# Top-ten stage and decoder layer in one program block; three weights scaled during the experts

## The chip, the cores and the metric

The kernel runs on 1 core of one Trainium2 chip. The metric is device time in microseconds, the median of several executions; less is better. One execution of the kernel was also recorded by the hardware profiler, and the rows below come from it.

## The reference

Four layers are applied one after the other to x of shape (16, 128, 256), with a context of the same shape, all in float32:

```
x = L0(x, ctx)   # self-attention, cross-attention (16 heads), then a mixture of experts: top 2 of 8
x = L1(x, ctx)   # per batch: score every row, take the ten best, attend from them to ctx,
                 #   write the ten results back in place of the ten rows
x = L2(x, ctx, mask)   # decoder layer:
    h, kv = rmsnorm(x, ln1), rmsnorm(ctx, ln1)
    q, k, v = h @ Wq, kv @ Wk, kv @ Wv          # 16 query heads, 4 key heads of 64
    q, k = rope(q), rope(k)
    hidden = x + softmax(q k^T / 8 + mask) v @ Wo
    x = hidden + (silu(n @ Wgate) * (n @ Wup)) @ Wdown,   n = rmsnorm(hidden, ln2)
x = L3(x, ctx)   # attention with ternary weights, residual
```

The gain ln1 multiplies the rows of Wq, Wk and Wv, and ln2 those of Wgate and Wup. The kernel multiplies these weights by their gains once, in SBUF, and then norms rows by their root mean square alone.

## The kernel before

The kernel is written by hand: every engine (PE, ACT, DVE, POOL, SP) has its own list of instructions, kept in order by counting semaphores. A `with nc.Block(...)` opens a stretch in which each engine runs its own function; at its end the engines meet. `end_turn()` (L244) adds an `all_engine_barrier` (L246) that also clears the semaphores so that their counts start again from zero. The stages:

- Self-attention and cross-attention of L0 with the router between them (block at L644). Its scatter of row ids is 32 indirect DMAs from POOL (L1292).
- Experts (block at L1434): 39 blocks of 128 rows. SP streams 2 MB of weights for each block and, at blocks 8, 13, 18, 23 and 28 (`grouped_at`), loads five of the decoder's six weights. POOL gathers the rows of block j + 2 (L1142) and scatters the results of block j - 2 (L1150), both indirect DMAs.
- Top-ten stage (block at L1632): four groups g of four batches. For each group PE computes `scores`, DVE takes `maxima`, PE turns the maxima, DVE subtracts them from the queries, PE computes `scores_turned`, ACT takes `exps`, PE computes `products`, DVE divides, PE makes `rows_out`, DVE adds a bias, PE's `put_back` spreads the ten rows and DVE's `replace` writes them into `xres`. Two PSUM banks serve the small jobs in the order of the list `in_turn`: a job's bank must have been read out (`tok_claim`) before the next job on it starts. POOL only multiplies four weights by their gains in this stage (L1658). SP loads the experts' rows, then `wq2`, and, once the last `products` are done, the mask (L1651). `end_turn()` follows.
- Decoder layer (block at L2080): a pipeline over 16 batches in slots t. Batch b's input stage is `stats_in` (DVE), `rms_in` (POOL), `scale_in` (DVE), `turn_in` (PE), `in_copy` (ACT), `queries` twice and `keys_values` (PE), `rope_queries`, `rope_keys` (DVE), `values` (ACT), and `rope_sums` (POOL). It runs in slots t = -3 to -1 for the first batches, with nothing else beside it. Then `scores` of batch 0 (L2096) opens slot 0. `end_turn()` follows.
- L3's attention, and the stores.

Of the kernel before, what the change touches and what calls it, by code (L numbers as in the profile page):

```python
# [17 lines left out]
P = 128  # L18
# [46 lines left out]
def build(nc, A, out):  # L65
    with ExitStack() as ctx:
# [72 lines left out]
        def view(at, shape):  # L139
# [3 lines left out]
            if len(shape) == 1:  # L143
# [63 lines left out]
        mask2 = w_sa[:, :, :].rearrange("p c n -> p (c n)").rearrange("p (b k) -> p b k", b=B)  # L207
# [9 lines left out]
        ld = {n: sem("ld_" + n) for n in ("x", "ctx", "small", "sa", "ca", "l1", "l3", "l2", "ids", "xn", "mask", "fc2b")}  # L217
# [10 lines left out]
        names = ["s_full", "st_full", "mt_full", "nd_full", "a_full", "b_full", "c_full", "a_free", "b_free", "c_free", "max_ok", "sub_ok", "p_ok", "o_ok",  # L228
                 "row_full", "row_ok", "bv_ok", "bias_ok", "pad_ok", "hx_ok", "hc_ok", "q_full0", "q_full1", "q_free0", "q_free1", "chain", "pchain", "const", "stats", "rstd_ok", "xn_ok",
                 "cn_ok", "summed", "divided", "scaled", "values_ok", "scored", "masked", "shifted", "maxed", "probs", "turned", "pt_ok", "biased",  # L230
                 "multiplied", "roped", "act_ok", "fc1_full", "fc1_free", "fc2_full", "y_ok",
                 "turned_in", "xb_ok", "routed", "picked_in", "taken", "measured", "keys_ok",
                 "counted", "scattered", "xs_ok", "colb_ok", "gat_ok", "exp_ok", "gates_ok",
                 "s0_full", "s1_full", "s2_full", "s3_full", "s0_free", "s1_free", "s2_free", "s3_free",
                 "stats_mid", "rstd_mid", "mid_ok",
                 "row_stats", "rows_ok", "chosen_ok", "rows_at", "totals", "ids_ok", "tables", "moe_chain", "kv_full", "kv_free", "tok_qk_ok",
                 "tok_b_full", "tok_c_full", "tok_b_free", "tok_c_free", "tok_colb_ok", "tok_gat_ok", "tok_p_ok", "tok_s_full", "tok_max_ok", "tok_mt_full", "tok_sub_ok", "tok_st_full", "tok_o_ok", "tok_nd_full", "tok_put_full", "tok_bv_ok", "tok_pad_ok", "tok_chain", "put_full", "late_rstd"]
# [93 lines left out]
        def load_grouped(sp, n):  # L331

            tile = {"wq2": wq2, "wkv2": wkv2, "wo2": wo2, "wg2": wg2, "wu2": wu2, "wd2": wd2}[n]
            sp.dma_start(tile, A[n].rearrange("(c p) n -> p c n", p=P)).then_inc(ld["l2"], 16)
# [1296 lines left out]

        with nc.Block(no_gpsimd_drain=True) as block:  # L1632
            @block.sync
            def _(sp):
# [24 lines left out]

            @block.tensor  # L1660
            def _(pe):
# [139 lines left out]
                for g in range(G):  # L1801
                    if g > 0:
                        put_back(g - 1)
                    maxima_turned(g)
                    if g + 1 < G:
                        score_rows(g + 1)
                    scores_turned(g)
                    if g + 1 < G:
# [7 lines left out]
                    products(g)  # L1816
                    if g + 1 < G:
# [10 lines left out]
            def _(act):  # L1828
# [60 lines left out]
                for g in range(G):  # L1889
                    exps(g)  # L1890
                    if g + 1 < G:
# [14 lines left out]
            def _(dve):  # L1906
                link = chained(dve, M["tok_chain"])

# [76 lines left out]
                def replace(g):  # L1985
                    dve.wait_ge(M["tok_put_full"], g + 1)
                    for j in range(GB):
                        b = g * GB + j
                        nc.vector.scalar_tensor_tensor(out=xres[:, b, :], in0=xres[:, b, :], scalar=keep[:, b:b + 1],
                                                       in1=S[j][:, 0:D], op0=ALU.mult, op1=ALU.add)  # L1990
# [9 lines left out]
                for g in range(G):  # L2000
# [16 lines left out]
        A4 = H // NKV  # L2017
        w2 = 12288
        masked_tile = SP
        turned_probs = PT  # L2020
        roped_q = view(w2, [2, 2, A4, P])
        roped_k = view(w2 + 2048, [2, 2, P])
        values2 = view(w2 + 2560, [2, NKV, HD])
        normed_in = view(w2 + 3072, [2, 2, D])
        normed_inT = view(w2 + 4096, [2, 2 * C, P])
        normed_mid = view(w2 + 5120, [D])
        normed_midT = view(w2 + 5376, [C, P])
        gated = view(w2 + 5632, [FC, P])
        heads_out = view(w2 + 6656, [FC, P])
        q_cos, q_sin = [w_ca[:, c, :].rearrange("p (h a n) -> p h a n", h=2, a=A4) for c in range(2)]  # L2030
        k_cos, k_sin = [w_l1[:, 0, k * D:(k + 1) * D].rearrange("p (h n) -> p h n", h=2) for k in range(2)]
        st_mid, mv_mid, ve_mid, rstd_mid = small[:, 0:6], small[:, 6:8], small[:, 8:9], small[:, 9:10]

        SLOT_JOBS = [("wo", -1, "a"), ("qa", 1, "b"), ("qb", 1, "c"), ("kv", 1, "a"), ("xt", -1, 0), ("at", 2, 1),
                     ("g0", -1, 2), ("u0", -1, 3), ("g1", -1, 0), ("u1", -1, 1), ("pv0", 0, "a"), ("pv1", 0, "b"), ("d", -1, "c")]
        JOB_BANK = {0: banks[0], 1: banks[1], 2: banks[2], 3: banks[3], "a": banks[5], "b": banks[6], "c": banks[7]}
        JOB_FULL = {0: M["s0_full"], 1: M["s1_full"], 2: M["s2_full"], 3: M["s3_full"],
                    "a": M["a_full"], "b": M["b_full"], "c": M["c_full"]}
        JOB_FREE = {0: M["s0_free"], 1: M["s1_free"], 2: M["s2_free"], 3: M["s3_free"],
                    "a": M["a_free"], "b": M["b_free"], "c": M["c_free"]}  # L2040
        job_at, n_jobs = {}, {h: 0 for h in JOB_BANK}
        for t in range(-2, B + 1):
            for name, ahead, home in SLOT_JOBS:
                if 0 <= t + ahead < B:
                    job_at[name, t + ahead] = (home, n_jobs[home])
                    n_jobs[home] += 1

        def job_claim(pe, name, b):

            home, k = job_at[name, b]  # L2050
            if k > 0:
                pe.wait_ge(JOB_FREE[home], k)
            if home in range(4) and 0 <= slot_of(name, b) < B:
                pe.wait_ge(M["masked"], 4 * slot_of(name, b) + home + 1)
            return JOB_BANK[home]

        def slot_of(name, b):
            return b - next(ahead for n, ahead, _ in SLOT_JOBS if n == name)

        def job_done(name, b):  # L2060
            return JOB_FULL[job_at[name, b][0]]

        def job_moved(name, b):
            return JOB_FREE[job_at[name, b][0]]

        def await_done(eng, name, b):

            home, k = job_at[name, b]
            eng.wait_ge(JOB_FULL[home], k + 1)
            return JOB_BANK[home]  # L2070

        def await_job_moved(eng, name, b):

            home, k = job_at[name, b]
            eng.wait_ge(JOB_FREE[home], k + 1)

        def is_batch(b):
            return 0 <= b < B

        with nc.Block(no_gpsimd_drain=True) as block:  # L2080
            @block.tensor
            def _(pe):

                def scores(b):
                    pe.wait_ge(M["roped"], 4 * (b + 1))
                    if b > 0:
                        pe.wait_ge(M["masked"], 4 * b)
# [10 lines left out]
                    ins.then_inc(M["scored"], 1)  # L2098
# [456 lines left out]
```

## Time and profile before

| | us |
|---|---|
| median of 3 runs | 1445.94 (1444.47 to 1445.95) |
| the profiled execution: its own time / its span | 1450.84 / 1449.1 |
| PE busy in the span | 1298.5 (90%) |
| DVE / ACT / POOL busy | 677.1 / 621.4 / 427.8 |

Starts are microseconds from the start of the span. PE means matmuls, PEld the loading of their weights, SPq, POOLq and so on the sequencers of these engines. What stands in brackets behind a row is the idle time of that engine before it and whose instruction ended it. A row of a window has its start and end, its length, the busy time and count of PE, PEld, DVE, ACT and POOL, the granted clock of PE (1.00 is 2.4 GHz, 0.50 is 1.2 GHz), the busy share of the DMA engines and GB/s. By start times the experts end and the top-ten stage begins at 679; its last instruction starts at 818.36; the decoder's first at 830.30; L3's attention begins at about 1283.

### The profile page before, as it was taken

What the parts mean: (1) busy time and instruction counts of PE and PEld (TensorE: products, weight loads), DVE (VectorE), ACT (ScalarE), POOL (GpSimd) and SP (SyncE); (2) the same over time, 40 slices, a digit from 0 to 9 for tenths busy, and PEclk for the clock granted to TensorE, in tenths of its full rate; (3) what the DMA queues carried; (4) which work ended last, traced back from release to release, by engine and by line L of the source; (5) the groups of instructions that cost most, each with busy time, mean ns of one, the idle gap of its engine ahead of it and who ended that gap; (6) DMA issues with size and microseconds to landing.
All of it is one profiled execution on the core that took longest, in us unless ns stands there. A gap on an engine that the chain in (4) does not pass through costs nothing. (4 is left out here: it accounts for less than half of the span.)

```text
span 1449.1 us, 34173 instructions
## 1 busy us (share of the span) xinstructions
PE 1298.5 (90%) x13946; PEld 1058.8 (73%) x13946; DVE 677.1 (47%) x1457; ACT 621.4 (43%) x1444; POOL 427.8 (30%) x549
## 2 busy tenths in 40 slices
PE   4899999976899999999687379999999999788997
PEld 2566666655689999997566268888888888666665
DVE  3676777766322000001753255455464453336666
ACT  2444555421545455553121046455455565334442
POOL 3224445253223222221500044334334242132200
PEclk9999999997899999999567589999999999999999
DMA  8000000000589999996300100000000000000000
GB/s 293 2 2 2 2 2 16 9 16 23 157 294 333 339 354 351 356 332 211 101 2 2 30 1 1 2 2 1 1 1 1 2 1 1 1 1 2 17 16 31
DMA packets 80042, 120.11 MB, mean 83 GB/s; under 512 B 12112, under 2 KB 62544, under 8 KB 79760
## 3 DMA queue, kind: packets, MB, share of 16 engines
q1 hardware_dynamic: 73840, 106.62, 21.9%
q0 software_dynamic: 4768, 10.26, 2.0%
q8 instruction: 112, 1.84, 0.5%
q10 hardware_dynamic: 1280, 1.04, 0.2%
q14 instruction: 42, 0.34, 0.1%
HBM read 108.43 MB, written 9.48 MB: 81 GB/s over the span
## 5 line engine op out<-in xcount | busy, mean ns | idle before, releaser
L1529 ACT ACTIVATE w_ca<-scores,fc1b 128x128 f32<-128x128 f32 x312 | 114.3, 367 | 140.1 <-PE scores L1484 118.9
L921 ACT ACTIVATE reg<-scores 128x1024 f32<-128x1024 f32 x96 | 93.0, 1021 | 168.8 <-PE scores L688 151.1
L1484 PEld LDWEIGHTS scores<-reg 128*128 128x128 f32 x1248 | 146.7, 194 | 6.9 <-DMA reg<-in_fc 2.7
L1484 PE MATMUL scores<-reg 128*128 128x128 f32 x1248 | 147.7, 277 | 3.6 <-DMA reg<-in_fc 1.5
L1494 PE MATMUL bank<-reg,w_ca 128*128 128x256 f32 x624 | 141.1, 379 | 0.3 <-DVE small L1554 0.3
L1015 DVE TENSOR_REDUCE reg<-scores 128x8 f32<-128x1024 f32 x96 | 113.0, 1219 | 57.9 <-PE scores L678 49.6
L2215 ACT ACTIVATE reg<-reg,mx 128x128 f32<-128x128 f32 x256 | 99.1, 389 | 83.8 <-DVE mx L2395 83.4
L1563 DVE TENSOR_TENSOR reg<-bank,reg 128x256 f32<-128x256 f32 x39 | 16.6, 425 | 241.4 <-PE bank L1494 226.4
L2304 POOL TENSOR_TENSOR reg<-reg,rden 128x512 f32<-128x512 f32 x64 | 66.5, 1040 | 210.7 <-DVE rden L2400 210.6
L1494 PEld LDWEIGHTS bank<-reg,w_ca 128*128 128x128 f32 x624 | 115.6, 190 | 14.5 <-DVE small L1554 0.3
L2131 PE MATMUL scores<-reg 128*128 128x128 f32 x1024 | 122.3, 279 | 0.5 <-ACT reg L2238 0.5
L2131 PEld LDWEIGHTS scores<-reg 128*128 128x128 f32 x1024 | 119.7, 196 | 0.7 <-ACT reg L2238 0.7
L2124 PE MATMUL bank<-reg 128*128 128x256 f32 x512 | 118.8, 385 | 0.8 <-issue 0.8
L2124 PEld LDWEIGHTS bank<-reg 128*128 128x128 f32 x512 | 94.7, 190 | 26.6 <-issue 13.2
L1036 DVE RECIPROCAL reg<-bank 128x256 f32<-128x256 f32 x48 | 84.2, 1754 | 33.2 <-PE bank L703 30.0
L861 ACT ACTIVATE reg<-bank,qk_bias,shape_c 128x512 f32<-128x512 f32 x96 | 69.5, 778 | 56.4 <-PE bank L661 56.0
L1150 POOL DMA_INDIRECT expert_out<-reg,block_ids_of x39 | 38.5, 986 | 151.5 <-DVE reg L1563 85.6
L2131 PE MATMUL bank<-reg 128*128 128x128 f32 x640 | 78.2, 279 | 0.7 <-ACT reg L2245 0.7
L2131 PEld LDWEIGHTS bank<-reg 128*128 128x128 f32 x640 | 76.5, 195 | 1.9 <-ACT reg L2245 1.1
L2422 DVE TENSOR_TENSOR reg<-scores,reg 128x512 f32<-128x512 f32 x32 | 22.1, 692 | 109.8 <-PE scores L2131 109.8
L688 PEld LDWEIGHTS scores<-reg 32*128 32x128 f32 x1536 | 48.2, 189 | 30.5 <-issue 30.4
L678 PEld LDWEIGHTS scores<-reg 32*128 32x128 f32 x1536 | 48.7, 188 | 29.2 <-ACT reg L921 22.9
(272 smaller groups left out, 2324.3 us busy)
## 6 DMA issues: line engine op xcount, KB each, us to landing
reg<-in_fc SPq DMA_DIRECT2D x78, 1024.0 KB
reg<-expert_out SPq DMA_DIRECT2D x16, 256.0 KB, 3.0
xres<-in_x SPq DMA_DIRECT2D x4, 512.0 KB, 11.3
ctxr<-in_ctx SPq DMA_DIRECT2D x1, 2048.0 KB, 15.5
w_l<-in_w_l SPq DMA_DIRECT2D x2, 1024.0 KB, 12.5
routed_rows<-reg SPq DMA_DIRECT2D x8, 256.0 KB
out<-xres SPq DMA_DIRECT2D x8, 256.0 KB, 2.6
w_sa<-in_w_sa SPq DMA_DIRECT2D x1, 1024.0 KB, 8.4
```

What stands on the lines that cost most here:

```text
L678: ins = nc.tensor.matmul(S[r][:, (2 * s + c) * P:(2 * s + c + 1) * P], Qs[rows_of(r), (b // GB) % 2, s, c, batch(b)], Ks[rows_of(r), (b // ...
L861: ins = nc.scalar.activation(dst[:, g % 2, s, m, :], bank[:, :], ACT.Identity, scale=scale[:, s:s + 1], bias=bias[:, s, m:m + 1])
L921: ins = nc.scalar.activation(PT2[:, t % 2, 2 * half:2 * half + 2, :, :, :].rearrange("p r s c q -> p (r s c q)"), scores4[:, 2 * half:2 * ...
L1015: ins = nc.vector.tensor_reduce(mxpad.rearrange("p (c n d) -> p n c d", c=C, d=DH)[:, 4 * half:4 * half + 4, :, 0], scores4[:, 2 * half:2 ...
L1036: link(nc.vector.reciprocal(rd, banks[4][:, 2 * P:4 * P]))
L1484: ins = nc.tensor.matmul(S[n % 4][:, 0:P], up_w8[j % 2][:, c, f * P:(f + 1) * P], xbT[:, j % 2, c, :], start=(c == 0), stop=(c == C - 1))
L1494: ins = nc.tensor.matmul(T[j % 2][:, 0:D], h1[:, j % 2, f, :], down_w8[j % 2][:, f, :], start=(f == 0), stop=(f == FC - 1))
L1529: nc.scalar.activation(h1[:, j % 2, f, :], S[n % 4][:, 0:P], ACT.Gelu, bias=fc1b[:, bass.ds(e * FC + f, 1)]).then_inc(M["fc1_free"], 1)
L2124: ins = nc.tensor.matmul(bank[:, 0:D], src[:, f, :], w[:, f, :], start=(f == 0), stop=(f == FC - 1))
L2131: ins = nc.tensor.matmul(bank[:, k * P:(k + 1) * P], w[:, c, w0:w0 + P], src[:, c, :], start=(c == 0), stop=(c == C - 1))
L2215: ins = nc.scalar.activation(v[:, a, :], v[:, a, :], ACT.Exp, bias=cols_of(mx, n)[:, a:a + 1], accum_out=cols_of(psum, n)[:, a:a + 1])
L2304: nc.gpsimd.tensor_tensor(v, v, spread(rden, n), ALU.mult).then_inc(M["scaled"], 1)
```

## The change

1. The decoder's functions move into the top-ten stage's block, behind it on each engine; the block's end and `end_turn()` between them go. So the decoder gets semaphores of its own (`l2_...`), and PE waits for the last `replace` (`tok_back`) before `scores` of batch 0.
2. The input stage of batches 0 and 1 and the queries, keys and values of batch 0 are made inside the top-ten stage: `stats_in` of batches 0 to 2 in group 2, `scale_in` of 0 and 1 at its end, and the rest in group 3. Five jobs are put into `in_turn` ahead of the last `y`. Some tiles get other places for this (`normed_in`, `q_cos`, `gated`, the mask).
3. `wkv2`, `wg2` and `wu2` are multiplied by their gains on POOL in the experts' blocks 33 to 35; only `wq2` stays in the top-ten stage.
4. The mask's load moves to just behind the load of `wq2`.

```diff
-        mask2 = w_sa[:, :, :].rearrange("p c n -> p (c n)").rearrange("p (b k) -> p b k", b=B)
+        mask2 = view(0, [B, P])
...
+        gains_at = {33: (wkv2, "ln1"), 34: (wg2, "ln2"), 35: (wu2, "ln2")}
...  # experts, gpsimd, inside the loop over j, behind gather_rows and scatter_rows
+                    if j in gains_at:
+                        w, gain = gains_at[j]
+                        pool.wait_ge(ld["l2"], 16 * len(grouped_at))
+                        for c in range(C):
+                            nc.gpsimd.tensor_scalar(w[:, c, :], w[:, c, :], col(gain, c), None, ALU.mult).then_inc(M["tok_gains"], 1)
...
+            if g + 1 == G:
+                in_turn += [("at", 0), ("at", 1), ("qa", 0), ("qb", 0), ("kv", 0)]
             in_turn += [("y", g)]
...  # top-ten, sync
                 load_grouped(sp, "wq2")
+                sp.dma_start(mask2, A["mask"].rearrange("b q k -> q b k")).then_inc(ld["mask"], 16)
                 for g in range(1, G):
                     expert_rows_in(g)
-                sp.wait_ge(M["tok_nd_full"], G)
-                sp.dma_start(mask2, A["mask"].rearrange("b q k -> q b k")).then_inc(ld["mask"], 16)
...  # top-ten, gpsimd
-                pool.wait_ge(ld["l2"], 16 * 6)
-                for w, gain in ((wq2, "ln1"), (wkv2, "ln1"), (wg2, "ln2"), (wu2, "ln2")):
-                    for c in range(C):
-                        nc.gpsimd.tensor_scalar(w[:, c, :], w[:, c, :], col(gain, c), None, ALU.mult)
+                pool.wait_ge(ld["wq2"], 16)
+                for c in range(C):
+                    nc.gpsimd.tensor_scalar(wq2[:, c, :], wq2[:, c, :], col("ln1", c), None, ALU.mult).then_inc(M["tok_gains"], 1)
...  # top-ten, tensor
                     if g > 0:
                         put_back(g - 1)
+                    if g + 1 == G:
+                        l2_turn_in(pe, 0)
+                        l2_turn_in(pe, 1)
                     maxima_turned(g)
                     if g + 1 < G:
                         score_rows(g + 1)
+                    if g + 1 == G:
+                        pe.wait_ge(M["tok_gains"], 4 * C)
+                        l2_queries(pe, "qa", 0, 0)
                     scores_turned(g)
+                    if g + 1 == G:
+                        l2_queries(pe, "qb", 0, 1)
...
                     products(g)
+                    if g + 1 == G:
+                        l2_keys_values(pe, 0)
...  # top-ten, scalar
+                    if g + 1 == G:
+                        l2_in_copy(act, 0)
+                        l2_in_copy(act, 1)
                     exps(g)
+                    if g + 1 == G:
+                        l2_values(act, 0)
...  # top-ten, vector
+                    if g == G - 2:
+                        for b in range(3):
+                            l2_stats_in(dve, l2_link[0], b)
+                    if g + 1 == G:
+                        l2_rope_queries(dve, 0, 0)
+                        l2_rope_queries(dve, 0, 1)
                     divide(g)
...
                     out_rows(g)
+                    if g == G - 2:
+                        l2_scale_in(dve, 0)
+                        l2_scale_in(dve, 1)
+                    if g + 1 == G:
+                        l2_rope_keys(dve, 0)
                 replace(G - 1)
-        end_turn()
...
-        with nc.Block(no_gpsimd_drain=True) as block:
             @block.tensor
             def _(pe):
...
-                pe.wait_ge(ld["l2"], 16 * 6)
-                for t in range(-2, B + 1):
+                pe.wait_ge(M["tok_back"], 1)
+                pe.wait_ge(M["tok_o_ok"], G)
+                for t in range(B + 1):
...  # decoder, gpsimd: rope_sums, loop still from t = -3
+                    if b == 0:
+                        pool.wait_ge(M["tok_st_full"], 3)
+                        pool.wait_ge(M["tok_nd_full"], 3)
```

The functions `l2_turn_in`, `l2_queries`, `l2_keys_values`, `l2_in_copy`, `l2_values`, `l2_stats_in`, `l2_scale_in`, `l2_rope_queries` and `l2_rope_keys` are the decoder's own ones of before, with the same instructions, moved out so that both stages can call them.

## Rows read from the trace of the kernel before

**Rows 1.** Windows over the top-ten stage, the gap and the decoder.

```profile
680.00:820.00 140.00, 104.85 (x1839) 84.09 (x1838) 71.82 (x218) 27.57 (x45) 20.64 (x9) 0.68 0.16 48
820.00:846.00 26.00, 8.89 (x56) 8.13 (x60) 7.40 (x23) 1.58 (x3) 6.11 (x14) 0.63 0.00 1
846.00:1282.00 436.00, 419.98 (x3692) 368.56 (x3692) 207.39 (x474) 227.26 (x714) 151.01 (x243) 0.99 0.01 1
```

**Rows 2.** Timeline of all engines, from the last top-ten instruction to the decoder's first scores.

```profile
818.36 1.66 DVE L1989 SCALAR_TENSOR_TENSOR xres<-xres,reg,scores 128x256 f32<-128x256 f32 x4 [1.36 <-PE scores L1780]
...
830.30 0.43 DVE L2359 BATCH_NORM_STATS2 st<-xres 128x6 f32<-128x256 f32 x1 [10.29 <-PEq L246]
...
835.55 6.25 PE L2131 MATMUL bank<-reg 128*128 128x128 f32 x40 [0.69 <-ACT reg L2245]
...
845.76 3.59 PE L2096 MATMUL scores<-reg 32*128 32x128 f32 x64 [2.65 <-POOL reg L2327]
```

**Rows 3.** The barrier's line L246 in 815:835, count, min/median/max ns.

```profile
L246 POOLq DRAIN  x1: 9057/9057/9057, 820.3 to 820.3; - x1
```

**Rows 4.** The same line in 1200:1300, behind the decoder.

```profile
L246 POOLq DRAIN  x1: 34/34/34, 1282.1 to 1282.1; - x1
...
  DVE st L992: 1.4, 1
```

**Rows 5.** Timeline of PE in the last top-ten group.

```profile
799.11 7.05 PE L1744 MATMUL scores<-w_ca,reg 32*128 32x32 f32 x128 [2.19 <-DVE w_ca L1968]
808.22 1.93 PE L1759 MATMUL bank<-w_sa,reg 128*32 128x32 f32 x128 [2.06 <-ACT w_sa L1877]
...
814.68 1.86 PE L1772 MATMUL bank<-w_l,reg 128*128 128x256 f32 x4 [2.41 <-DVE reg L1976]
817.05 1.24 PE L1780 MATMUL scores<-reg 32*128 32x256 f32 x8 [0.52 <-DVE reg L1983]
```

**Rows 6.** Timeline of PE, the same shapes and the decoder's projections elsewhere.

```profile
790.36 1.10 PE L1772 MATMUL bank<-w_l,reg 128*128 128x256 f32 x4 [1.31 <-DVE reg L1976]
...
863.22 2.07 PE L2096 MATMUL scores<-reg 32*128 32x128 f32 x64
...
868.77 3.73 PE L2131 MATMUL bank<-reg 128*128 128x128 f32 x32
```

**Rows 7.** Windows: the decoder's first projections, and the last `scores_turned`.

```profile
799.00:806.00 7.00, 6.89 (x128) 6.89 (x128) 0.06 (x1) 0.00 (x0) 0.00 (x0) 0.50 0.01 2
...
835.50:839.00 3.50, 3.45 (x17) 3.45 (x18) 0.62 (x2) 0.00 (x0) 0.68 (x1) 0.53 0.00 0
```

**Rows 8.** Timeline of DVE in groups 2 and 3, and of its input stage.

```profile
788.00 1.76 DVE L1975 RECIPROCAL reg<-bank 128x256 f32<-128x256 f32 x1 [15.08 <-PE bank L1764]
...
793.34 2.36 DVE L1958 TENSOR_REDUCE reg<-scores 128x8 f32<-128x1024 f32 x2 [1.41 <-PE scores L1726]
...
812.31 1.76 DVE L1975 RECIPROCAL reg<-bank 128x256 f32<-128x256 f32 x1 [13.25 <-PE bank L1764]
...
833.01 0.35 DVE L2369 TENSOR_SCALAR reg<-xres,rstd 128x256 f32<-128x256 f32 x1 [1.68 <-POOL rstd L2298]
```

**Rows 9.** Timeline of ACT in group 3.

```profile
806.23 1.94 ACT L1877 ACTIVATE w_sa<-scores 128x1024 f32<-128x1024 f32 x2 [15.64 <-PE scores L1744]
```

**Rows 10.** Timeline of POOL: block 35's scatter, the last gather, the four weights' gains.

```profile
647.16 0.99 POOL L1150 DMA_INDIRECT expert_out<-reg,block_ids_of  x1 [3.32 <-DVE reg L1563]
650.13 0.96 POOL L1142 DMA_INDIRECT reg<-routed_rows,block_ids_of  x1 [1.98 <-PE bank L1473]
...
690.98 20.40 POOL L1658 TENSOR_SCALAR reg<-reg,cols 128x1024 f32<-128x1024 f32 x8 [10.74 <-DMA reg<-in_wq]
```

**Rows 11.** PE timeline: the last gathered block is turned. DMA view: a scatter's landing.

```profile
663.48 0.38 PE L1473 MATMUL bank<-ident,reg 128*128 128x128 f32 x2
...
expert_out<-reg,block_ids_of POOLq DMA_INDIRECT x39, 5.9
```

**Rows 12.** Window: the experts' rows and wq2 arriving.

```profile
688.00:690.00 2.00, 1.81 (x9) 1.25 (x7) 1.43 (x4) 0.75 (x2) 0.00 (x0) 1.00 0.98 390
```

More of the change, by code:

```diff
@@ L214, in build @@
         Q = banks[6:8]
-        ld = {n: sem("ld_" + n) for n in ("x", "ctx", "small", "sa", "ca", "l1", "l3", "l2", "ids", "xn", "mask", "fc2b")}
+        ld = {n: sem("ld_" + n) for n in ("ctx", "small", "sa", "ca", "l1", "l3", "l2", "wq2", "ids", "xn", "mask", "fc2b")}
         stored = sem("stored")
@@ L1630, in keys_of @@
             return slice(j * P, (j + 1) * P)
+        A4 = H // NKV
+        w2 = 12288
+        masked_tile = SP
+        turned_probs = PT
+        roped_q = view(w2, [2, 2, A4, P])
+        roped_k = view(w2 + 2048, [2, 2, P])
+        values2 = view(w2 + 2560, [2, NKV, HD])
+        normed_in = view(2048, [2, 2, D])
+        normed_inT = view(3072, [2, 2 * C, P])
+        normed_mid = view(w2 + 3072, [D])
+        normed_midT = view(w2 + 3328, [C, P])
+        k_cos, k_sin = [view(w2 + 3584 + D * k, [2, P]) for k in range(2)]
@@ new lines, in build @@
+        q_cos, q_sin = [view(w2 + 4096 + 1024 * k, [2, A4, P]) for k in range(2)]
+        gated, heads_out = [w_ca[:, c, :].rearrange("p (f n) -> p f n", f=FC) for c in range(2)]
+        st_mid, mv_mid, ve_mid, rstd_mid = small[:, 0:6], small[:, 6:8], small[:, 8:9], small[:, 9:10]
+        SLOT_JOBS = [("wo", -1, "a"), ("qa", 1, "b"), ("qb", 1, "c"), ("kv", 1, "a"), ("xt", -1, 0), ("at", 2, 1),
+                     ("g0", -1, 2), ("u0", -1, 3), ("g1", -1, 0), ("u1", -1, 1), ("pv0", 0, "a"), ("pv1", 0, "b"), ("d", -1, "c")]
@@ new lines, in build, with job_claim @@
+        IN_TOP_TEN = [("at", 0), ("at", 1), ("qa", 0), ("qb", 0), ("kv", 0)]
+        for t in range(-2, B + 1):
+            for name, ahead, home in SLOT_JOBS:
+                if 0 <= t + ahead < B and (name, t + ahead) not in IN_TOP_TEN:
+                    job_at[name, t + ahead] = (home, n_jobs[home])
+                    n_jobs[home] += 1
+        def job_claim(pe, name, b):
+            if (name, b) in IN_TOP_TEN:
+                return tok_claim(pe, (name, b))
+            home, k = job_at[name, b]
+            if k == 0 and home in ("a", "c"):
+                h = tok_bank.index(JOB_BANK[home])
+                pe.wait_ge(tok_free[h], sum(1 for n in tok_at if tok_at[n][0] == h))
+            if k == 0 and home == "b":
+                pe.wait_ge(M["tok_sub_ok"], G)
+            if k > 0:
+                pe.wait_ge(JOB_FREE[home], k)
+            if home in range(4) and 0 <= slot_of(name, b) < B:
+                pe.wait_ge(M["l2_masked"], 4 * slot_of(name, b) + home + 1)
+            return JOB_BANK[home]
@@ new lines, in slot_of, with job_done, job_moved, await_done @@
+        def slot_of(name, b):
+            return b - next(ahead for n, ahead, _ in SLOT_JOBS if n == name)
+        def job_done(name, b):
+            if (name, b) in IN_TOP_TEN:
+                return tok_done((name, b))
+            return JOB_FULL[job_at[name, b][0]]
+        def job_moved(name, b):
+            if (name, b) in IN_TOP_TEN:
+                return tok_moved((name, b))
+            return JOB_FREE[job_at[name, b][0]]
+        def await_done(eng, name, b):
+            if (name, b) in IN_TOP_TEN:
+                return tok_await(eng, (name, b))
+            home, k = job_at[name, b]
+            eng.wait_ge(JOB_FULL[home], k + 1)
+            return JOB_BANK[home]
@@ new lines, in await_job_moved, with is_batch, l2_project @@
+        def await_job_moved(eng, name, b):
+            if (name, b) in IN_TOP_TEN:
+                return tok_await_moved(eng, (name, b))
+            home, k = job_at[name, b]
+            eng.wait_ge(JOB_FREE[home], k + 1)
+        def is_batch(b):
+            return 0 <= b < B
+        cos = [rope[:, 0, :].unsqueeze(1).to_broadcast([P, n, P]) for n in (A4, 2)]
+        sin = [rope[:, 1, :].unsqueeze(1).to_broadcast([P, n, P]) for n in (A4, 2)]
+        def l2_project(pe, name, b, w, w0s, src):
+            bank = job_claim(pe, name, b)
+            for k, w0 in enumerate(w0s):
+                for c in range(C):
+                    ins = nc.tensor.matmul(bank[:, k * P:(k + 1) * P], w[:, c, w0:w0 + P], src[:, c, :],
+                                           start=(c == 0), stop=(c == C - 1))
+            return ins
@@ new lines, in l2_queries, with l2_keys_values @@
+        def l2_queries(pe, name, b, half):
+            await_job_moved(pe, "at", b)
+            l2_project(pe, name, b, wq2, [(2 * a + half) * P for a in range(A4)], normed_inT[:, b % 2, 0:C, :])\
+                .then_inc(job_done(name, b), 1)
+        def l2_keys_values(pe, b):
+            bank = job_claim(pe, "kv", b)
+            for k in range(2):
+                for c in range(C):
+                    nc.tensor.matmul(bank[:, k * P:(k + 1) * P], wkv2[:, c, k * P:(k + 1) * P], normed_inT[:, b % 2, C + c, :],
+                                     start=(c == 0), stop=(c == C - 1))
+            for c in range(C):
+                ins = nc.tensor.matmul(bank[:, D:2 * D], normed_inT[:, b % 2, C + c, :], wkv2[:, c, D:2 * D],
+                                       start=(c == 0), stop=(c == C - 1))
+            ins.then_inc(job_done("kv", b), 1)
@@ new lines, in l2_turn_in, with l2_values @@
+        def l2_turn_in(pe, b):
+            pe.wait_ge(M["l2_xn_ok"], b + 1)
+            bank = job_claim(pe, "at", b)
+            for k in range(2):
+                for c in range(C):
+                    ins = nc.tensor.transpose(bank[:, (C * k + c) * P:(C * k + c + 1) * P],
+                                              normed_in[:, b % 2, k, c * P:(c + 1) * P], ident[:])
+            ins.then_inc(job_done("at", b), 1)
+        def l2_values(act, b):
+            bank = await_done(act, "kv", b)
+            if b == 0:
+                act.wait_ge(M["tok_st_full"], 3)
+            if b >= 2:
+                await_done(act, "pv1", b - 2)
+            nc.scalar.activation(values2[:, b % 2, :, :], bank[:, D:2 * D].rearrange("p (h d) -> p h d", d=HD), ACT.Copy)\
+                .then_inc(M["l2_values_ok"], 1)
@@ L2028, in build @@
[L2028 to L2035, printed above, removed]
@@ L2260, in out_copy @@
                         .then_inc(job_moved(f"pv{q}", b), 1)
-                for t in range(-2, B + 1):
+                for t in range(B + 1):
                     now, before_now, after_now = is_batch(t), is_batch(t - 1), is_batch(t + 1)
@@ L2345, in _ @@
             def _(dve):
[L2346 to L2348 removed]
+                link = l2_link[0]
                 def add_rows(name, b):
@@ L2425, in _ @@
                 dve.wait_ge(ld["mask"], 16)
-                for t in range(-3, B + 2):
+                for t in range(B + 2):
                     now, before_now, after_now = is_batch(t), is_batch(t - 1), is_batch(t + 1)
```

277 lines of the change are left out of this document (102 added, 175 removed).

## Prediction

> **What bounds the kernel now.** Read the windows by stage first [rows 1]. In the decoder PE is busy 419.98 of 436.00 us at a granted clock of 0.99: it is the bound there, and the change gives PE the same matmuls. In the top-ten stage PE is busy 104.85 of 140.00 us, all other engines less: a chain through PE, DVE and ACT sets the time. From 820 to 846 PE is busy 8.89 of 26.00 us and nothing else is busier: that stretch is what the change attacks.
>
> Next the timeline of all engines there [rows 2]. The last `replace` ends at 818.36 + 1.66 = 820.02. DVE's next instruction starts 10.29 us later, held by the barrier. Then the input stage of the first batches runs as a bare chain, and `scores` of batch 0 start at 845.76. So 845.76 - 820.02 = 25.74 us lie between the two stages: 10.28 of barrier and 15.46 of filling.
>
> Third, what the barrier consists of [rows 3]: POOL's DRAIN takes 9.06 us of it. The barrier behind the decoder, at the same line, has a DRAIN of 0.03 us, and DVE goes on after 1.4 us [rows 4]. So the 9 us don't belong to a barrier as such. What differs: the one at 820 is the first DRAIN that POOL executes behind its indirect DMAs (32 of the router, 39 gathers, 39 scatters); behind it POOL issues none. By 820 POOL had been idle since 711.38, the end of the gains [rows 10].
>
> **Part 1, one block.** It removes this barrier, 10.28 us. But one stays behind the decoder, and now that is the first behind the indirect DMAs. I take it that the DRAIN's 9.06 us move there, exposed as at 820, because all engines meet before it: its 0.03 becomes 9.06, +9.03. The ends: 0, if the 9 us belong to the place, and +9.03. Of the two I take the upper one, as nothing in the rows ties the time to the place and one thing ties it to what went before.
>
> The Trainium skill (page "VectorE: DVE Perf Modes", section "The DRAIN you can't avoid") says that the DRAINs of a kernel's boilerplate take about 12 ns, constant, on all five engines. The POOL row of 9057 ns is far from it [rows 3], that of 34 ns near [rows 4]. By this rule nothing would come back behind the decoder, and the gain would be 9 us more than by the row. The measurement decides for the row; rival (a) has the same outcome.
>
> **Part 2, the input stage inside the top-ten stage.** It removes the 15.46 us of filling. What it adds, place by place:
>
> DVE, group 2: `stats_in` of three batches is twelve small instructions. I bound them by the first at 0.43 us each, 5.2 us [rows 2]; 15.08 us of idleness stand before `divide` [rows 8]. Nothing. POOL's `rms_in` is free there. `scale_in` of two batches, 4 x 0.35 = 1.4 us [rows 8], stands between `out_rows` and `maxima`, where DVE is idle 1.41 us: nothing, with no reserve.
>
> PE, group 3: eight transposes before `maxima_turned`. The eight matmuls of the decoder's projections at full clock take 8 x 0.117 = 0.9 us [rows 6], and PE is idle 2.19 us before `scores_turned` [rows 5], in part because DVE does `replace` first. Nothing. Then `qa`, 16 matmuls, in the same idle time. At full clock 16 x 0.117 = 1.9 us; at 1.2 GHz the decoder's first projections ran 17 in 3.50 us, 0.206 each, so 3.3 us [rows 7]. PE has 2.19 - 0.9 = 1.3 us left: `scores_turned` start 0.6 to 2.0 us later. I take 2.0, as the clock stood at 0.50 through all of `scores_turned` [rows 7].
>
> `qb` lies in the 2.06 us in which PE waits for `exps` [rows 5]: 1.9 us fits, 3.3 costs 1.2. I take 0.6. `kv`, eight matmuls of 128 and four of 256 columns, lies in the 2.41 us before `rows_out` [rows 5]; at full clock it takes 8 x 0.117 + 4 x 0.23 = 1.9 us (0.23 as twice 0.117), at half clock 3.5 us and then costs 1.1. I take 0.5.
>
> ACT: two `in_copy` lie in 15.64 us of idleness [rows 9]; nothing. DVE: four `rope_queries` of the projections' results lie in the 13.25 us before the last `divide` [rows 8]; nothing. `rope_keys` lies in the 1.36 us before `replace` [rows 2]; its two instructions of 256 columns are bounded by 2 x 0.43; nothing. POOL's `rope_sums` ends behind `rope_keys` while DVE still does `replace` (1.66 us): nothing. The new wait of PE on `tok_back` holds nothing that could go earlier: behind it stand `scores`, which need the same PSUM banks. I take 0.2 us from the end of `replace` to the first matmul.
>
> The clock can pay this back. The same instructions at half and full clock [rows 5, 6]: `rows_out` 1.86 against 1.10, `scores` 3.59 [rows 2] against 2.07. In group 3 PE now has more to do between its waits, so the clock falls later or not at all: between 0 and 0.76 + 1.52 = 2.3 us for these two, and for `scores_turned`, never at full clock here, between 0 and half of 7.05, 3.5. I take half of each, 2.9 us. Added 2.0 + 0.6 + 0.5 + 0.2 = 3.3; given back 2.9; the net is +0.4, between -5.0 (0.6 + 0.2 - 2.3 - 3.5) and +4.5 (2.0 + 1.2 + 1.1 + 0.2).
>
> The Trainium skill (page "TensorE: Matmul & The Clock Gate", section "Part 1: The HAM clock gate") says that the slow clock is the default and sustained activity releases it. It would put the net at the lower end, -5.0 and 1424.7 in all, since `qa` and `qb` are dense work; the rows show 0.50 over a `scores_turned` with PE busy 6.89 of 7.00 us [rows 7], so being busy alone did not raise it.
>
> **Part 3, gains during the experts.** The eight instructions took 20.40 us for seven halves of 1024 columns, 2.9 us each [rows 10]; `wkv2` is 2.9, `wg2` and `wu2` 5.8 us each. In the top-ten stage they were off the path: PE waited for none. In the experts they stand before the next gather. The last is the tightest: block 35's scatter, at 647.16 before, comes some 0.4 us later, the gains of `wu2` follow for 5.8 us and gather 38 is issued at about 654.3 instead of 650.13. It is needed when PE turns its rows at 663.48 [rows 11], 9.2 us later. I count nothing; without this cover a late gather stalls PE by as much as it is late. The weights' loads themselves are where they were. In the top-ten stage POOL no longer works beside DVE from about 697 to 711; I take nothing for that, between -2 and 0.
>
> **Part 4, the mask.** 1 MB more, behind `wq2` and before the rows of group 1. Group 0's rows are issued before it, but arrive beside `wq2` while the DMA engines are busy 0.98 at 390 GB/s [rows 12]: 1 MB at that rate is 2.7 us. The first scores of the top-ten stage wait for these rows. SP itself issues one DMA more before group 1's rows, which are needed only after group 0's; nothing else stands behind it on SP. I take 0.5, between 0 and 2.7.
>
> **Sum.** -25.74 + 9.03 + 0.4 + 0.5 = -15.8 us. The profiled execution took 1450.84 us, 1.74 more than its span; it becomes 1435.0. It lies 4.9 us above the median of the runs, 1445.94, and the gain is in fixed waits, so the median becomes 1430.1.
>
> **Rivals.** (a) The DRAIN doesn't come back: -15.8 - 9.0 = -24.8, 1421.1. For it: the decoder's POOL work then lies between the indirect DMAs and the DRAIN, and whatever it waits for may have passed. Against it: at 820 the gains and over 100 us of idleness lay between, and it still took 9 us. (b) The DRAIN moves, and the work put into group 3 runs at the slow clock with nothing paid back and the mask in full: -25.74 + 9.03 + 4.5 + 2.7 = -9.5, 1436.4. For it: the clock of 0.50 in `scores_turned`. Against it: the projections' own window shows 0.53 and their 40 matmuls together took 6.25 us [rows 2], less than 40 x 0.206, so the clock rose within them. (c) The moved gains stall the experts, and the kernel gets slower. Gather 38 has 9.2 us from issue to need; its transfer may take the 5.9 us of a scatter, as large [rows 11], so 3.3 remain. The gains are 14.5 us in all. If beside the DMA stream POOL took k times as long, the last gather would be late by at most 14.5 (k - 1) - 3.3: it eats the 15.8 us from k = 2.3, and at k = 3 the time is 1445.94 - 15.8 + 25.7 = 1455.8. For it: their time beside the matmuls' and DMAs' traffic is not in any row. Against it: beside a busy DVE they took 2.9 us each.
>
> **Chances.** The forecast (DRAIN moves, net near zero): 0.70. (a) 0.14, (b) 0.12, (c) 0.03; 0.01 for no change. The range reaches from rival (a)'s time to just short of (b)'s: 1420 to 1436. A measurement of this kernel tells 0.2%, 2.9 us, from no change. Faster: 0.70 + 0.14 + 0.12 = 0.96; same 0.01; slower 0.03.
>
> **What would show it.** In the profile of the changed kernel: no barrier between `replace` and `scores`, and under 1 us between them; a POOL DRAIN of about 9 us at the barrier behind the decoder, and L3's attention starting about 16 us earlier than at 1283 (25 if rival (a) holds and the DRAIN is short). `scores_turned` of group 3 starting 0.6 to 2.0 us later after `put_back`; if the clock column reads 1.00 there, the lower end of the net holds. The experts' end at the same time as before, within 0.5 us; if it is later, (c). If the gap between `replace` and `scores` is over 3 us, a wait that I took as covered isn't: POOL's `rope_sums`, or `out_rows` behind `qb`'s bank.

## The result and the profile after

The changed kernel took 1425.24 us (median, 1423.89 to 1428.53), the kernel before, on the same chip, 1445.2 (1440.54 to 1445.95): ratio 0.9872, 95% interval 0.9844 to 0.9900, 20.0 us less. The forecast was 1430.1 us, 15.8 less. The profiled execution of the changed kernel took 1426.36 us with a span of 1424.5.

Timeline of the changed kernel, all engines, where [rows 2] showed the gap: the last `replace`, then `scores` of batch 0. Columns as there.

```profile
807.10 1.66 DVE L2170 SCALAR_TENSOR_TENSOR xres<-xres,reg,scores 128x256 f32<-128x256 f32 x4 [0.18 <-PE scores L1945]
...
808.81 3.06 PE L2223 MATMUL scores<-reg 32*128 32x128 f32 x64 [1.78 <-DVE xres L2170]
```

`replace` ends at 808.76 and PE goes on at 808.81. Of the 25.74 us between the stages 0.05 are left. The barrier's line behind the decoder, in 1200:1300, answers to [rows 4]:

```profile
L237 POOLq DRAIN  x1: 9057/9057/9057, 1246.1 to 1246.1; - x1
...
  DVE st L983: 10.3, 1
```

The DRAIN has moved there at its full 9057 ns, and DVE now waits 10.3 us instead of 1.4. The last top-ten group answers to [rows 5]:

```profile
790.27 0.71 PE L1945 MATMUL scores<-reg 32*128 32x256 f32 x8 [2.54 <-DVE reg L2139]
790.91 1.09 PE L1741 MATMUL bank<-ident,reg 128*128 128x128 f32 x8
791.84 0.38 PE L1899 MATMUL bank<-ident,reg 128*128 128x128 f32 x2
792.35 2.02 PE L1716 MATMUL bank<-reg 128*128 128x128 f32 x16
794.30 3.77 PE L1909 MATMUL scores<-w_ca,reg 32*128 32x32 f32 x128
798.00 2.05 PE L1716 MATMUL bank<-reg 128*128 128x128 f32 x16
800.13 1.26 PE L1924 MATMUL bank<-w_sa,reg 128*32 128x32 f32 x126
...
802.23 1.16 PE L1729 MATMUL bank<-reg 128*128 128x128 f32 x8
803.22 1.03 PE L1732 MATMUL bank<-reg 128*128 128x256 f32 x4
804.70 1.10 PE L1937 MATMUL bank<-w_l,reg 128*128 128x256 f32 x4 [0.45 <-DVE reg L2157]
806.32 0.71 PE L1945 MATMUL scores<-reg 32*128 32x256 f32 x8 [0.52 <-DVE reg L2164]
```

Each added job (L1741 the transposes, L1716 `qa` and `qb`, L1729 and L1732 `kv`) stands where PE was idle. Their matmuls of 128 columns took 0.126 to 0.145 us each (a group's time by its count), at a granted clock of 1.00. What came after ran at that clock too: `scores_turned` took 3.77 us instead of 7.05. Windows of 2 us over PE (busy time and count, clock, DMA share, GB/s) show why. In the kernel before, PE did little ahead of `scores_turned` (799.11), and the clock fell:

```profile
794.00:796.00 2.00, 0.16 (x4) 1.00 0.00 0
796.00:798.00 2.00, 0.93 (x10) 0.95 0.00 0
798.00:800.00 2.00, 0.89 (x18) 0.50 0.00 0
```

In the changed kernel PE is busy there, and the clock falls only behind the wait for the last `replace`, within the decoder's first `scores` (808.81):

```profile
792.00:794.00 2.00, 1.88 (x18) 1.00 0.03 8
794.00:796.00 2.00, 2.00 (x65) 1.00 0.00 0
...
808.00:810.00 2.00, 1.19 (x36) 0.92 0.00 0
810.00:812.00 2.00, 2.00 (x37) 0.50 0.04 8
```

The gains on POOL were one block of 20.40 us in [rows 10]. Two of the three weights that moved, among the gathers and scatters of the experts (timeline of POOL, blocks 34 to 36):

```profile
636.72 5.68 POOL L1459 TENSOR_SCALAR reg<-reg,cols 128x1024 f32<-128x1024 f32 x2
642.57 1.01 POOL L1133 DMA_INDIRECT reg<-routed_rows,block_ids_of  x1 [0.17 <-issue]
643.88 1.01 POOL L1141 DMA_INDIRECT expert_out<-reg,block_ids_of  x1 [0.30 <-issue]
644.93 5.69 POOL L1459 TENSOR_SCALAR reg<-reg,cols 128x1024 f32<-128x1024 f32 x2
650.79 1.03 POOL L1133 DMA_INDIRECT reg<-routed_rows,block_ids_of  x1 [0.18 <-issue]
```

The profiled executions cut at the same instructions (starts and ends from the timelines, in us):

| stretch | before | after | difference |
|---|---|---|---|
| start to the experts' first block | 386.61 | 384.01 | -2.60 |
| experts | 291.19 | 289.63 | -1.56 |
| to group 3's first `put_back` | 118.04 | 116.63 | -1.41 |
| to the end of the last `replace` | 24.18 | 18.49 | -5.69 |
| to `scores` of batch 0 | 25.74 | 0.05 | -25.69 |
| to the decoder's last instruction on DVE | 436.01 | 436.95 | +0.94 |
| to L3's first | 1.37 | 10.33 | +8.96 |
| to the end of the span | 165.96 | 168.41 | +2.45 |

In the profiles of the kernels below the start takes 379.5 to 389.2, the experts 289.4 to 295.1, the decoder 433.2 to 440.4 and the last stretch 165.9 to 168.7 us, though their edits hardly touch these stretches. The third stretch takes 116.45 to 118.81 us in those whose top-ten stage is the changed kernel's up to there. So the differences in the first three rows and in the decoder's and the last are no shown effects of the change. What repeats in both profiles of the changed kernel is 18.49, 0.05 and 10.33.

### The profile page after: what moved, and what is told of

It reads as the page before. It is cut to its first block and busy times, and to the rows that moved or that the text cites. A ratio compares the mean times of both kernels' runs of the same rounds, so it can differ in the third digit from the quotient of the medians.

```text
span 1424.5 us, 34151 instructions
## 1 busy us (share of the span) xinstructions
PE 1292.7 (91%) x13946; PEld 1057.5 (74%) x13946; DVE 673.3 (47%) x1457; ACT 621.6 (44%) x1444; POOL 428.5 (30%) x549
## 5 line engine op out<-in xcount | busy, mean ns | idle before, releaser
L1491 PE MATMUL bank<-reg,w_ca 128*128 128x256 f32 x624 | 141.1, 380 | 0.3 <-DVE small L1551 0.3
L1491 PEld LDWEIGHTS bank<-reg,w_ca 128*128 128x128 f32 x624 | 115.8, 191 | 14.3 <-DVE small L1551 0.3
L1716 PE MATMUL scores<-reg 128*128 128x128 f32 x1024 | 122.4, 279 | 0.5 <-ACT reg L2330 0.5
L1716 PEld LDWEIGHTS scores<-reg 128*128 128x128 f32 x1024 | 119.8, 196 | 0.7 <-ACT reg L2330 0.7
L2251 PE MATMUL bank<-reg,w_ca 128*128 128x256 f32 x512 | 118.8, 386 | 0.8 <-issue 0.8
L2251 PEld LDWEIGHTS bank<-reg,w_ca 128*128 128x128 f32 x512 | 94.9, 190 | 26.4 <-issue 13.2
L2474 DVE TENSOR_TENSOR w_ca<-scores,w_ca 128x512 f32<-128x512 f32 x32 | 22.1, 692 | 109.8 <-PE scores L1716 109.8
L669 PE MATMUL scores<-reg 32*128 32x128 f32 x1536 | 59.9, 295 | 11.2 <-ACT reg L912 10.8
L679 PE MATMUL scores<-reg 32*128 32x128 f32 x1536 | 57.7, 287 | 12.4 <-DVE reg L1006 12.4
```

The costliest lines, as they stand in the source:

```text
L669: ins = nc.tensor.matmul(S[r][:, (2 * s + c) * P:(2 * s + c + 1) * P], Qs[rows_of(r), (b // GB) % 2, s, c, batch(b)], Ks[rows_of(r), (b // ...
L679: ins = nc.tensor.matmul(S[r][:, (2 * s + c) * P:(2 * s + c + 1) * P], Ks[rows_of(r), (b // GB) % 2, s, c, batch(b)], Qs[rows_of(r), (b // ...
L1491: ins = nc.tensor.matmul(T[j % 2][:, 0:D], h1[:, j % 2, f, :], down_w8[j % 2][:, f, :], start=(f == 0), stop=(f == FC - 1))
L1716: ins = nc.tensor.matmul(bank[:, k * P:(k + 1) * P], w[:, c, w0:w0 + P], src[:, c, :], start=(c == 0), stop=(c == C - 1))
L2251: ins = nc.tensor.matmul(bank[:, 0:D], src[:, f, :], w[:, f, :], start=(f == 0), stop=(f == FC - 1))
```

## The experiments

All ratios are to the kernel before, timed on the same chip, with their 95% intervals. Three groups of four kernels ran, each with the kernel before beside it: `after_again`, `after_drain`, `before_drain` and `after_nofill` (before: 1452.85 us); `qa_late`, `warm`, `warm_drain` and `drains` (1450.92); `gains_late`, `mask_late`, `warm2_drain` and `drains2` (1449.71). The changed kernel ran in the first group alone; those of the other groups are set beside it by their ratios.

**after_again**: the changed kernel once more.

> The changed kernel itself, beside the others on one chip. Both theories: about 20 us under the kernel before, as in its first runs (1425.24 against 1445.2).

Measured: 1430.31 us, 0.9843 (0.9823 to 0.9863), 22.5 us less. With the first result the gain is 20 to 23 us.

**after_drain**: is it the place or what went before?

```diff
                 # top-ten, gpsimd, behind the gains of wq2
+                nc.gpsimd.drain()
```

> The changed kernel with one more DRAIN on POOL, behind the gains of wq2, where POOL is idle for about 75 us. Theory A (the 9 us belong to the first DRAIN behind indirect DMAs): the new DRAIN takes about 9.06 us under cover, the one of the barrier behind the decoder 0.03 us, and the kernel is 9 us faster than the changed one, 29 under before. Theory B (they belong to the barrier's place, or to the first barrier): the barrier keeps its 9.06 us and the time stays that of the changed kernel.

Measured: 1420.54 us, 0.9801 (0.9764 to 0.9838), 9.8 us under `after_again`; but the runs spread from 1414.77 to 1433.18 us and the two intervals overlap, so it is the profile that decides. The barrier behind the decoder, the new DRAIN, and the gains ahead of it:

```profile
L237 POOLq DRAIN  x1: 41/41/41, 1246.4 to 1246.4; - x1
...
  DVE st L983: 1.4, 1
...
L1824 POOLq DRAIN  x1: 14917/14917/14917, 688.4 to 688.4; - x1
...
688.46 5.78 POOL L1823 TENSOR_SCALAR reg<-reg,cols 128x1024 f32<-128x1024 f32 x2 [11.48 <-DMA reg<-in_wq]
```

The new DRAIN also counts the gains that run while it waits. They end at 688.46 + 5.78 = 694.24, it ends at 703.3: 9.1 us of its own. Decoder's end to L3 takes 1.40 us again. Theory A holds and B falls.

**before_drain**: the same line behind the four gains in the kernel before.

> The kernel before with the same DRAIN behind the four gains in the top-ten stage. Theory A: its barrier at 820 shrinks from 10.3 to about 1.4 us and the kernel gets 9 us faster (ratio 0.994). Theory B: no change.

Measured: 1446.17 us, 0.9962 (0.9943 to 0.9982), 6.7 us less. The gap between the stages is 17.30 us instead of 25.74, 8.4 less, with a DRAIN of 41 ns in it. The last group took 25.01 us instead of 24.18 in this profile, so 7.6 us remain of it, within the interval of the time (2.6 to 8.3 us less). The 9 us expected were too many by little.

**drains and drains2**: what sets the 9 us?

```diff
                 # drains: behind the router's last scatter; drains2: experts, block 8, behind the memset
+                nc.gpsimd.drain()
                 # both: behind the gains of wq2 (in drains twice)
+                nc.gpsimd.drain()
```

> The changed kernel with a DRAIN on POOL behind the router's 32 indirect DMAs, and two more, one behind the other, behind the experts' 78 (after the gains of wq2). Theory A1 (9 us for the first DRAIN behind any indirect DMAs): about 9, 9 and 0.03 us, the work that runs ahead of each not counted. A2 (only the first DRAIN of the program): 9, 0.03, 0.03. A3 (so much for each DMA): 2.6, 6.4, 0.03.

> The changed kernel with a DRAIN on POOL in the experts' block 8 (50 indirect DMAs behind it) and one behind the gains of wq2 (60 more). If the time goes by the number of indirect DMAs since the last DRAIN (9.06 / 110 = 0.082 us each, as the 6.4 us behind 78 suggest), the second takes 60 x 0.082 = 4.9 us behind the gains; if it is fixed, 9; if it goes by what is still in flight, near 0.

Measured: 1424.92 and 1415.65 us, of one execution each, so no gain is read from them. The table has the DRAIN's end less the end of POOL's instruction ahead of it:

| DRAIN | indirect DMAs since the last one | us | us per DMA |
|---|---|---|---|
| before, after: barrier | 110 | 9.06 | 0.082 |
| drains: behind the gains of wq2 | 78 | 6.4 | 0.082 |
| drains2: behind the gains of wq2 | 60 | 5.0 | 0.083 |
| drains: the one right behind it | 0 | 0.05 | |
| drains: behind the router's last DMA | 32 | 7.8 | |
| drains2: block 8 | 50 | 6.0 | |

```profile
693.47 5.67 POOL L1825 TENSOR_SCALAR reg<-reg,cols 128x1024 f32<-128x1024 f32 x2 [10.79 <-DMA reg<-in_wq]
...
L1826 POOLq DRAIN  x1: 12174/12174/12174, 693.4 to 693.4; - x1
...
L1827 POOLq DRAIN  x1: 53/53/53, 705.6 to 705.6; - x1
```

```profile
687.57 5.67 POOL L1824 TENSOR_SCALAR reg<-reg,cols 128x1024 f32<-128x1024 f32 x2 [10.50 <-DMA reg<-in_wq]
...
L1825 POOLq DRAIN  x1: 10704/10704/10704, 687.5 to 687.5; - x1
```

Where POOL had issued no DMA for over 10 us the time goes by their number, 0.082 us each. So the "first DRAIN behind indirect DMAs" of the prediction named the right one but not its price: A3 holds for these, not A1, and A2 falls too, since each DRAIN with new DMAs before it costs again. The bytes don't set it: one of the router's DMAs moves 128 pairs of ids, one of the experts' 128 rows of 256 numbers, and the router's 32 still make up 9.06 - 6.4 = 2.7 us, as much for each as the others. The two DRAINs in the midst of DMAs, 7.8 and 6.0 us, took longer than by this rule (2.6 and 4.1 us); that they also wait for transfers in flight fits, but was not tested. Why a DMA that has long landed costs time in a later DRAIN stays open.

**after_nofill**: one block, but the input stage where it was.

```diff
-                in_turn += [("at", 0), ("at", 1), ("qa", 0), ("qb", 0), ("kv", 0)]
...  # all l2_ calls in the top-ten functions go as well
-                for t in range(B + 1):
+                for t in range(-2, B + 1):
```

> The changed kernel without its input stage in the top-ten stage: one block and no barrier, but the decoder's input stage of batches 0 and 1 runs behind the last replace as before. My terms: barrier removed 10.3, DRAIN back 9.0, and some 1.5 us from the gains' leaving: 2 to 3 us under before. Rival (the barrier's removal was the gain, the filling was cheap or hidden anyway): over 8 us under before. From replace to the first scores I expect about 15.5 us, and the slow clock in the last group's scores_turned again (7.05 us).

Measured: 1452.05 us, 1.0001 (0.9987 to 1.0015): nothing. Replace to scores takes 16.69 us, 9.05 less than before, and the barrier behind the decoder 8.96 more; the last group takes 24.48 us, as before the change. By itself the joining of the blocks earns nothing, since nearly all of the barrier was DRAIN and that is only put off. The 2 to 3 us expected were too much: the filling takes 16.7 us when it starts without a barrier, not 15.5, and the 1.5 us for the leaving of the gains didn't come (see `gains_late`).

**qa_late**: what kept the clock up?

```diff
-                        pe.wait_ge(M["tok_gains"], 4 * C)
-                        l2_queries(pe, "qa", 0, 0)
                     scores_turned(g)
                     if g + 1 == G:
+                        pe.wait_ge(M["tok_gains"], 4 * C)
+                        l2_queries(pe, "qa", 0, 0)
                         l2_queries(pe, "qb", 0, 1)
```

> The changed kernel with qa moved from before scores_turned to behind it, next to qb. Theory A (qa's dense work before scores_turned is what kept the clock at 2.4 GHz): the last group's scores_turned runs at the slow clock again, 7.05 us instead of 3.77, and from put_back to the end of replace it takes 22 to 26 us instead of 18.49. Rival B (the eight transposes were enough, or the clock was luck): scores_turned stays at 3.8 us and the stretch at about 18.3.

Measured: 1432.82 us, 0.9876 (0.9845 to 0.9906). The last group takes 22.58 us instead of 18.49, in the range of A:

```profile
796.04 5.00 PE L1909 MATMUL scores<-w_ca,reg 32*128 32x32 f32 x128 [1.31 <-DVE w_ca L2148]
800.98 5.82 PE L1716 MATMUL bank<-reg 128*128 128x128 f32 x32
806.73 1.26 PE L1924 MATMUL bank<-w_sa,reg 128*32 128x32 f32 x126
```

`scores_turned` took 5.00 us, between A's 7.05 and B's 3.8: the clock fell later than before, within it (at about 798.3). The transposes alone hold the clock for part of it; `qa` ahead of it makes the rest. That split rests on one profile. The larger reading does not: `scores_turned` of group 3 took 3.77 us in all seven profiles with `qa` ahead of it and nothing else changed in the group (the two of the changed kernel, `after_drain`, `drains`, `drains2`, `gains_late`, `mask_late`), and 7.05 us in all three without the filling (the kernel before, `before_drain`, `after_nofill`). The intervals of this kernel and the changed one overlap; the 4.1 us are the profile's.

**warm, warm_drain, warm2_drain**: does the same help the other groups?

```diff
+                def keep_warm(n, k=6):   # results read by nobody
+                    for _ in range(n):
+                        nc.tensor.matmul(banks[k][:, C * P:2 * C * P], ident[:], w_l1[:, 0, 0:C * P], start=True, stop=True)
                 for g in range(G):
+                    keep_warm(5)
                     ...
                         score_rows(g + 1)
+                        keep_warm(4, 4)          # warm2_drain only
                     ...
                 put_back(G - 1)
+                keep_warm(3, 4)                  # warm2_drain only
```

> The changed kernel with five superfluous matmuls of 128x256 (2.3 us at the fast clock) before put_back and maxima_turned in every top-ten group, where PE is idle about 2.5 us; their results are read by nobody. Theory A (the clock falls because of these idle stretches, and the top-ten stage is bound by PE at 1.2 GHz): scores_turned of groups 1 and 2 go from 7.05 to about 3.8 us, and the stage loses 8 to 12 us. Rival B (the narrow matmuls lower the clock whatever stands before them): no gain, and up to 2 us lost in group 0, where the filler runs at the slow clock and takes 4 us.

> Both together: the filler matmuls and the hidden DRAIN. If both theories A hold, 9 us under the filler kernel and some 40 under the kernel before.

> Hidden DRAIN and filler matmuls, and now also four of them between score_rows and scores_turned and three behind the last put_back. If it is the idle stretches before scores_turned that lower the clock, scores_turned of groups 1 and 2 go from 5.66 and 5.12 us to about 3.8 and the stage loses another 4 to 8 us; if they stay at 5 us, the work after them lowers it.

Measured: 1427.64 us, 0.9830 (0.9796 to 0.9865); 1413.08, 0.9722 (0.9694 to 0.9750); 1401.89, 0.9678 (0.9653 to 0.9702). The time of `warm` alone isn't told from the changed kernel's (0.9872 and 0.9843); that of `warm2_drain` lies clear under `after_drain`'s (0.9801), which has the same DRAIN. `scores_turned` of the four groups, timeline of PE, in the changed kernel, in warm and in warm2_drain:

```profile
707.70 7.05 PE L1909 MATMUL scores<-w_ca,reg 32*128 32x32 f32 x128
732.87 7.05 PE L1909 MATMUL scores<-w_ca,reg 32*128 32x32 f32 x128 [1.75 <-DVE w_ca L2149]
763.76 7.05 PE L1909 MATMUL scores<-w_ca,reg 32*128 32x32 f32 x128 [1.08 <-DVE w_ca L2149]
794.30 3.77 PE L1909 MATMUL scores<-w_ca,reg 32*128 32x32 f32 x128
```

```profile
717.65 3.77 PE L1909 MATMUL scores<-w_ca,reg 32*128 32x32 f32 x128 [0.53 <-DVE w_ca L2154]
738.18 5.66 PE L1909 MATMUL scores<-w_ca,reg 32*128 32x32 f32 x128 [1.75 <-DVE w_ca L2154]
764.90 5.12 PE L1909 MATMUL scores<-w_ca,reg 32*128 32x32 f32 x128 [1.75 <-DVE w_ca L2154]
794.48 4.09 PE L1909 MATMUL scores<-w_ca,reg 32*128 32x32 f32 x128
```

```profile
705.87 4.00 PE L1910 MATMUL scores<-w_ca,reg 32*128 32x32 f32 x128
728.00 3.77 PE L1910 MATMUL scores<-w_ca,reg 32*128 32x32 f32 x128
751.50 3.77 PE L1910 MATMUL scores<-w_ca,reg 32*128 32x32 f32 x128
776.46 3.77 PE L1910 MATMUL scores<-w_ca,reg 32*128 32x32 f32 x128
```

From the experts' end to the last `replace` the changed kernel takes 135.1 us (134.9 to 137.3 in the profiles with the same stage), warm 127.9, warm2_drain 121.9. Superfluous work in all these idle places shortened the stage by 13.3 us, as it keeps the clock at 2.4 GHz for the work behind it. With only the place ahead of `put_back` filled, `scores_turned` of groups 1 and 2 ran partly at the slow clock, at 5.66 and 5.12 us instead of the 3.8 expected, and the stage lost 7.2 us instead of 8 to 12. Rival B falls. warm_drain is 37.8 us under the kernel before, as expected (some 40), and 14.6 under warm instead of 9; in its profile the barrier behind the decoder fell from 10.3 to 1.4 us, so 9 of them are the DRAIN; the intervals of the two times leave room for the rest to be chance. warm2_drain, with the hidden DRAIN, is the fastest kernel here: 47.8 us under the kernel before, about 24 under the changed one by the ratios (0.9678 against 0.9843).

**gains_late and mask_late**: part 3 undone, and part 4 in its place only (the mask's load behind the rows of all groups).

```diff
-        gains_at = {33: (wkv2, "ln1"), 34: (wg2, "ln2"), 35: (wu2, "ln2")}
+        gains_at = {}                    # gains_late: all four in the top-ten stage
                 load_grouped(sp, "wq2")
-                sp.dma_start(mask2, ...)
                 for g in range(1, G):
                     expert_rows_in(g)
+                sp.dma_start(mask2, ...)         # mask_late
```

> The changed kernel with all four gains back in the top-ten stage (part 3 undone). My term for part 3 was 0, between -2 and 0: this run within 2 us of the changed one. If the gains of the three weights slow DVE there, the stretch from the experts' end to the last put_back but one is 1 to 2 us longer than the 116.6 to 118.8 us of the changed kernel. Rival: the gains cost PE something in the experts; then the experts get shorter here than 289.6 us.

> The changed kernel with the mask loaded behind the rows of all groups (part 4 undone in its place only). My term for the mask was +0.5, between 0 and 2.7: this run 0 to 2.7 us faster in the first 30 us of the top-ten stage. Rival: no difference, since group 0's rows are ahead of the mask.

Measured: 1426.1 us, 0.9842 (0.9821 to 0.9862), and 1427.16, 0.9858 (0.9838 to 0.9878), both as the changed kernel. The stretch to group 3's `put_back` takes 116.64 and 116.72 us, against 116.63 in the changed kernel, the experts 289.8 us in both, with or without the gains. So the gains cost the experts nothing, and neither part 3 nor the mask's place ahead of the rows is worth anything measurable. The 0 to 2.7 us expected of `mask_late` didn't come; its rival holds.

## Why the prediction was right, and where a term was off

- **The gap, -25.74**: -25.69. Every wait taken as covered was: `rope_sums` ended at 807.87, before `replace` did (808.76), `scale_in` cost nothing with 0.36 us of idleness left, and PE waited 0.05 us on `tok_back`.
- **The DRAIN, +9.03**: +8.96, at the place and size forecast. after_drain shows that it goes by what POOL did before, drains and drains2 that it goes by the number of indirect DMAs; so rival (a) falls, whose ground was that what the DRAIN waits for might have passed by then. The Trainium skill (page "VectorE: DVE Perf Modes", section "The DRAIN you can't avoid") gives about 12 ns for the boilerplate DRAINs of the preamble and postamble. The prediction stretched that to this barrier, which is the kernel's own; its POOL DRAIN took 9057 ns in both places.
- **The net of group 3, +0.4 (from -5.0 to +4.5)**: the term that was mis-sized. The group's part is -5.69; with `scores` at 3.06 instead of 3.59 us, -0.53, it is -6.2, below its lower end. (In after_again these first `scores` took 2.07 us; the -5.69 is the same there.) Piece by piece from `put_back` on: `scores_turned` starts 0.76 later (forecast 2.0) and takes 3.28 less; the products before the last `divide` take 1.88 less, a clock term that was left out; `rows_out` 0.75 and `put_back` 0.53 less; `qb` and `kv` cost 0 (forecast 1.1). The step that failed: that `qa` would run at half clock, read off a clock of 0.50 in the old `scores_turned`. The clock had fallen there behind a stretch in which PE was busy 0.16 and 0.93 us of two windows of 2 us, and the change put work into just that stretch. So 7.0 us came back where 2.9 were forecast. The Trainium skill (page "TensorE: Matmul & The Clock Gate", section "Part 1: The HAM clock gate") has it that the slow clock is the default and that activity releases it, and by that the prediction would have put the net at its lower end, -5.0. The traces side with it: the clock stayed at 1.00 where the idle time was filled, and in `warm` it rose from 0.50 to 1.00 around the first filler.
- **Gains, 0, and mask, +0.5**: 0 and 0. Gather 38 was issued at 650.79, not 654.3, as the experts ran some 4 us earlier in that execution. The gains of `wg2` and `wu2` took 2.8 us an instruction also beside the experts, those of the half as wide `wkv2` 1.6. Rival (c) falls.
- **Rival (b)**: the slow clock in group 3 didn't come; qa_late shows what it would cost, 4.1 us, when the dense work stands behind instead of ahead.
- **The signs**: L3's attention began at 1256.09, 27 us earlier and not about 16, more than the 25 named as the sign of rival (a), though the DRAIN was at its full 9057 ns. 5.6 us of it are the first three rows of the table above, which vary from profile to profile, and 6 the net of group 3. A start in a single profile couldn't tell these two outcomes apart; the DRAIN's own row did. The experts' end, forecast within 0.5 us, came 4.2 us earlier for the same reason.

With the measured terms the sum is -25.69 + 8.96 - 6.2 = -22.9, against 20.0 and 22.5 timed. The mechanism of the two large terms was right. The forecast fell 4 to 7 us short of the gain by the clock term, and its range still held the result because it reached down to rival (a)'s time, which has another cause; that part was luck.

## What to carry to other kernels

A cost in a barrier may belong to what an engine did long before; ask what releases it, and where it will be paid once the barrier is gone. The DRAIN behind indirect DMAs cost nothing when it was given to POOL while POOL was idle. Where PE waited some 2 us between narrow matmuls, work moved into the wait was more than free here: it kept the clock up for the rest of the group. So price such work at the clock that it makes, not at the clock of the row before.

## What the runs showed of the hardware

- A POOL DRAIN took 0.082 to 0.083 us for each indirect DMA issued since the last one (60, 78 and 110 of them), and 0.03 to 0.05 us with none. For 110 of them it took 9057 ns both 140 us after the last DMA (the kernel before, 680 to 820) and 570 us after it, with the decoder's work of POOL between (the changed kernel, 676 to 1246).
- 128 matmuls of 32x32 took 7.05 us at 1.2 GHz and 3.77 at 2.4 GHz, though PE is shown as busy in either. PE being busy with them did not raise the clock (0.50 through all 7 us), while the clock that dense matmuls had left high stayed at 1.00 through the 3.77 us.
- Matmuls whose results nobody reads made the top-ten stage 13.3 us shorter in the profile (warm2_drain), at `scores_turned` of 3.77 to 4.00 us instead of 7.05 in groups 0 to 2.
